# GpSimd's first weight splits of the second MoE moved into the second cross-attention, and those of the first expert taken from it

## The reference

```
x = x + L0_xattn(layernorm(x), ctx)      # 16 heads, null key, 1024 keys
x = x + L0_attn(layernorm(x))            # self-attention, 4 heads, q and k RMS-normed
x = x + L0_ffn(layernorm(x))             # mW1 = W1 + sum_e g_e TW1[e]; gelu; mW2 likewise: 8 experts mixed
x = x + L1_xattn(layernorm(x), ctx)      # 16 heads of 16, keys = context and own
x = x + L1_attn(layernorm(x))            # Mamba2 (residual inside), then memory retrieval and a gate
x = x + L1_ffn(layernorm(x))             # MoE: argmax routing over 8 experts, 256 -> 1024 -> 256
```

## Time and profile before

| | us |
|---|---|
| median of 3 runs | 514.2 (513.56 to 514.58) |
| span of the profiled execution | 512.5 |
| TensorE busy | 484.9 |
| VectorE busy | 261.0 |
| ScalarE busy | 232.9 |
| GpSimd busy | 80.2 |

### The profile page before, as it was taken

How to read it: one execution, slowest core, us unless ns; L and a number is a source line. 1 busy time by engine, 2 the same in 40 slices (tenths; PEclk the granted TensorE clock), 3 DMA queues, 4 the chain that set the end, 5 groups by cost and what they waited for, 6 DMA issues and landing times.

```text
span 512.5 us, 8527 instructions
## 1 busy us (share of the span) xinstructions
PE 484.9 (95%) x3600; PEld 414.8 (81%) x3600; DVE 261.0 (51%) x443; ACT 232.9 (45%) x409; POOL 80.2 (16%) x64
## 2 busy tenths in 40 slices
PE   6999999999999999999878999999999879889997
PEld 6977989899989999999765769975666669678697
DVE  2737131337065141420445977765656586467585
ACT  1636333346255141421125876516666253237772
POOL 2111000001010000000240434300000160203442
PEclk9989999999999999999999999999999999999999
DMA  8557000022420000000495999910000092255000
GB/s 320 223 193 243 2 2 0 1 83 83 165 82 1 1 0 1 1 2 1 157 425 234 388 420 405 366 70 1 2 1 1 1 373 121 84 212 199 0 1 10
DMA packets 12325, 62.50 MB, mean 122 GB/s; under 512 B 1183, under 2 KB 3615, under 8 KB 6400
## 3 DMA queue, kind: packets, MB, share of 16 engines
q1 hardware_dynamic: 9696, 52.17, 26.0%
q0 software_dynamic: 2592, 9.80, 5.5%
HBM read 61.84 MB, written 0.13 MB: 121 GB/s over the span
## 4 chain that ended last, share of the span: by engine, by line
PE 65%; issue 17%; DVE 8%; POOL 4%; ACT 3%; DMA 1%; POOLq 1%; SPq 0%; DVEq 0%; ACTq 0%
PE W L1322 18%; PE W L1283 14%; PE W L1466 8%; PE W L1513 6%; PE W L1264 3%; PE W L1299 3%; POOL w_lo L489 3%; PE W L1220 2%; PE W L1344 2%; POOL small L497 1%; DVE scr L1086 1%; ACT w_hi L552 1%; PE W L1458 1%; PE W L1383 1%; PE W L1247 1%
## 5 line engine op out<-in xcount | busy, mean ns | idle before, releaser
L1322 PE MATMUL W<-probs_turned_hi,ctx_split_hi 128*128 128x256 f32 x256 | 72.8, 284 | 0.1
L1322 PE MATMUL W<-probs_turned_hi,ctx_split_lo 128*128 128x256 f32 x256 | 72.4, 283 | 0.0
L1322 PE MATMUL W<-probs_turned_lo,ctx_split_hi 128*128 128x256 f32 x256 | 72.4, 283 | 0.0
L869 DVE TENSOR_TENSOR probs_turned_lo<-W,probs_turned_hi 128x512 fp32r<-128x512 f32 x32 | 20.6, 685 | 65.0 <-ACT probs_turned_hi L602 65.0
L1513 PE MATMUL W<-w_hi,acts 128*128 128x256 f32 x272 | 50.9, 286 | 1.5 <-DVE acts L836 1.0
L1283 PE MATMUL W<-ctx_turned_hi,q_keys_hi 128*128 128x512 f32 x128 | 51.7, 404 | 0.0
L1283 PE MATMUL W<-ctx_turned_hi,q_keys_lo 128*128 128x512 f32 x128 | 50.6, 395 | 0.0
L1283 PE MATMUL W<-ctx_turned_lo,q_keys_hi 128*128 128x512 f32 x128 | 50.6, 395 | 0.0
L1322 PEld LDWEIGHTS W<-probs_turned_hi,ctx_split_hi 128*128 128x128 f32 x256 | 49.1, 192 | 0.8 <-DVE probs_turned_lo L869 0.5
L1322 PEld LDWEIGHTS W<-probs_turned_lo,ctx_split_hi 128*128 128x128 f32 x256 | 49.1, 192 | 0.2
L1322 PEld LDWEIGHTS W<-probs_turned_hi,ctx_split_lo 128*128 128x128 f32 x256 | 49.1, 192 | 0.0
(11 more groups left out here) (347 smaller groups left out, 901.6 us busy)
## 6 DMA issues: line engine op xcount, KB each, us to landing
arena<-units_dram SPq DMA_DIRECT2D x22, 1024.0 KB, 8.0
ctxmem<-units_dram SPq DMA_DIRECT2D x16, 1024.0 KB, 10.1
fixed<-units_dram SPq DMA_DIRECT2D x7, 1024.0 KB, 6.8
scr<-ctx_dram POOLq DMA_DIRECT2D x4, 512.0 KB, 3.7
pbuf<-ctx_dram POOLq DMA_DIRECT2D x4, 512.0 KB, 5.3
ctxmem<-ctxT_dram SPq DMA_DIRECT2D x2, 1024.0 KB, 14.7
ctxmem<-ctx_dram SPq DMA_DIRECT2D x2, 1024.0 KB, 14.1
scr<-ctxT_dram POOLq DMA_DIRECT2D x3, 512.0 KB, 6.4
```

The source lines that it names most:

```text
L869: dve.tensor_tensor(PT[1][at], bank(4 + c).rearrange("p (t m) -> p t m", t=4), f32(PT[0][at]), ALU.subtract).then_inc(ev("pl_sb"), 1)
L1322: mm = pe.matmul(ps, CXN[a][:, t, c * P:(c + 1) * P], PT[z][:, t, :], start=(t == 0 and n == 0), stop=(t == KEYT - 1 and n == 2))
```

## The change

- Halves 0 and 1 (`f1e0`) no longer belong to GpSimd. ScalarE makes both high parts after its copy of q and k (L652), where it made one; VectorE makes both low parts, put behind the normalization of the probabilities (L965) and ahead of its wait for the attention's output (L968).
- The four halves of `m1e0` and `m1e1` stay with GpSimd, but stand behind n = 5 (the second cross-attention) and not behind n = 6 and n = 7 (the Mamba stage).

```diff
 def hi_maker(p):
-    return "gpsimd" if p == 0 or MOE0 <= p < MOE0 + SLOTS else "scalar"
+    return "gpsimd" if MOE0 <= p < MOE0 + SLOTS else "scalar"
 def lo_maker(p):
-    return "gpsimd" if hi_maker(p) == "gpsimd" or p == 1 or (p % 4 == 3 and p > SLOTS) else "vector"
+    return "gpsimd" if hi_maker(p) == "gpsimd" or (p % 4 == 3 and p > SLOTS) else "vector"
...
-                if n == RSQRT_QK:
-
-                    keep_w(0, 0)
-                    keep_w(1, 0)
-                    keep_w(1, 1)
...
+                    for p in range(MOE0, MOE0 + SLOTS):
                         keep_w(0, p)
                         keep_w(1, p)
+                if n == 6:
+
+                    pool.memset(XP[:, :, :, 0:TAPS - 1], 0.0).then_inc(ev("xp_zero"), 1)
...
-            keep_w_hi("f1e0", [1])
+            keep_w_hi("f1e0")
...
             ins.then_inc(*tick("probsA"))
+            keep_w_lo("f1e0")
             dve.wait_ge(*made("outA_ps"))
```

More of the change, by code:

```diff
@@ L524, in _ @@
                             .then_inc(ev("pads_zero"), 1)
+                    for p in range(MOE0, MOE0 + SLOTS):
+                        keep_w(0, p)
+                        keep_w(1, p)
                 if n == 6:
                     pool.memset(XP[:, :, :, 0:TAPS - 1], 0.0).then_inc(ev("xp_zero"), 1)
[L528 to L532, removed]
                 if n == N_RSQRT - 1:
```

## The result

| | before | after |
|---|---|---|
| median, first comparison (4 runs each) | 514.39 us | 509.8 us (508.81 to 510.38) |
| ratio, 95% interval | | 0.989 (0.9852 to 0.9928) |
| median, second comparison (23 and 5 runs) | 514.24 us | 509.74 us (509.31 to 510.38) |
| ratio, 95% interval | | 0.9912 (0.9897 to 0.9928) |
| span of the profiled execution | 512.5 us | 508.8 us |

The changed kernel is faster. Its median is the forecast 509.8 us. Its interval is wide: it holds the forecast ratio of 0.9914, and the two medians of its own row differ by 4.6 us only. The second comparison gives 0.9%.

A forecast was written before the change was run, and what follows sets the result against it. Mostly TensorE bounds the kernel, but small VectorE and ScalarE steps, some held by GpSimd splits, do in self-attention and Mamba. Gains of 1.25 + 0 + 3.15 = 4.4 us take 514.2 to 509.8 us, range 509.0 to 511.9.

The forecast's parts named there:

- Part A: Self-attention: without GpSimd's splits, L958 gains 0.34 us and the pair L965 0.91, together 1.25 us; added work is hidden.
- that rival: First expert stage is bound by transfers and gives back the self-attention's 1.25 us: time 511.1 us, chance 0.08.
- Part B: Second cross-attention: the eight moved GpSimd instructions hold up nothing that matters, L1036 included; cost 0.
- The nearest row: Rival, second cross-attention: L1036 stands still once like the 8-column L1077, costing 1.4 us; time 511.2 us, chance 0.20.
- Part C: Mamba stage: with the splits gone, L1067, L1077, L1078 and the L1086 round are no longer held; gain 3.15 us.
- TensorE's filler: Mamba stage: filling products, late next after VectorE's chain, would take less than 0.1 us of the gain.
- the last sentence of part C: TensorE's granted clock is 1.00 and the changed places only lose idle time, so the clock adds nothing.
- the sum: Whole kernel: 1.25 us from self-attention, 0 from second cross-attention, 3.15 us from Mamba, together 4.4 us less.
- The rival of the other sign: Second cross-attention: every VectorE instruction touching SBUF stands still beside a split, losing 4.9 to 9.8 us; chance 0.02.

The follow-up runs named there:

- e5: Changed kernel with an added 8-column VectorE TENSOR_SCALAR ahead of L1030 in the first two steps of the second cross-attention: 511.42 us.
- e6: Changed kernel with an added 1-column VectorE TENSOR_SCALAR ahead of L1030 in the first two steps of the second cross-attention: 509.91 us.
- e11: Kernel before with more filling products, 22 for 17 in the self-attention and 22 for 12 in the Mamba stage: 514.1 us, ratio 0.9959.
- the first part alone: Kernel before with only the first expert's split moved from GpSimd to ScalarE and VectorE, second-layer splits left in the Mamba stage: 514.15 us, ratio 1.0002.
- e1: The changed kernel itself, timed more often beside the kernel before: 509.74 us, ratio 0.9912.
- e4: Changed kernel with the fourth half's two instructions put back behind n = 7: 508.8 us, ratio 0.9899.
- e8: Changed kernel with VectorE making all low parts of the second products of both expert stages, where GpSimd made every fourth: 508.6 us, ratio 0.986.
- e9: Kernel before with only the first expert's split moved to ScalarE and VectorE, plus 22 for 12 filling products in Mamba: 512.79 us, ratio 0.9945.
- e12: Changed kernel with GpSimd making no low parts but those of the four moved halves, VectorE all others: 506.36 us, ratio 0.982 of the kernel before.
- e7: Changed kernel with fewer filling products, 14 for 17 in the self-attention and 9 for 12 in the Mamba stage: 510.44 us, ratio 0.9891.

## Why the prediction was right in its steps and wrong in its size

- Part A: 1.25 us forecast, 1.25 measured. The additions on ScalarE and VectorE were hidden. The first expert stage gave nothing back (65.40 us in both), so that rival is out.
- Part B: 0 forecast, 0 measured (73.12 and 73.11 us). The nearest row would have cost 1.4 us; e5 and e6 show that its 8 columns were the reason it was held, and that one column is not. Shown.
- Part C: 3.15 us forecast, 3.22 measured; the 0.07 is L1061, at 0.35 us instead of 0.43. TensorE's filler is what is late next, as said.
- The step that failed is the last sentence of part C: TensorE's clock is 1.00 in the rows and "the two changed places only lose idle time, so no term for the clock". The row that I read is that of the first expert stage, not of the changed places, and it is one execution, which I took for every execution. The idle stretches that the change removes (1.3 us in the self-attention, 2.5 in Mamba) put the kernel before at risk of losing a part of TensorE's clock. It has mean clocks under 0.997 in 5 of 23, 6 of 13 and 15 of 23 executions of three comparisons, 1 to 5 us above the others. Longer fillers in these two stretches took away all its executions above 515 us (e11) and 1.8 us of its median, 515.92 to 514.1. The whole change closes both stretches, and none of its nine executions has a mean clock under 0.993.
- So a term was missing that has no fixed size: by the comparisons it is between 0.2 us of the median (514.24 us with, 514.0 without the executions of lower clock) and 1.8 us, and the range's lower end should have been near 508. That it made the first ratio 0.989 is likely but not shown: one of the four executions of before in it is at 515.89 us, where others had 0.990, but their clocks are not on record. With 23 executions, most of full clock, the gain is 4.5 us (0.9912), beside the 4.4 of the sum. That the median came out at 509.8 to the tenth is in part luck, since the changed kernel's own executions spread from 508.8 to 510.4 us with the clock from 24 to 31 us, for which the sum had no term either.
- The rival of the other sign (all of VectorE's work held) is out: maxima and copies beside the splits are as long as before.

What stays open: why the first part alone has a mean clock of 0.990 to 0.993 in all twelve executions and the kernel before, with the same idle stretch, only in some. The runs differ in when the stretch comes, and no run varied that alone. How often the kernel before loses it differs between the comparisons (5 of 23 with e1 to e4, 6 of 13 with e5 to e8, 15 of 23 with e9 to e12), which ran on three different chips; nothing here tells chip from chance. No execution of the kernel before at 515 us or more was profiled, so where it lost the clock is told by e11 and not by a trace. Nor is it shown what makes the low clock from 24 to 31 us shorter or longer between kernels that are the same there, nor what the rest of the 1.8 us is.

## What to carry to other kernels

Before work is given to GpSimd, look at what VectorE does beside it: an instruction with two SBUF inputs, or a TENSOR_SCALAR between SBUF tiles of more than one column, stood still here until GpSimd's ended, while PSUM sources, reductions and single columns passed. Move GpSimd's work beside the latter. An edit that shortens a wait of TensorE can have a second worth that one profile does not show: ask of every idle stretch in both versions whether the clock survives it in all executions, and never price two edits from runs of each alone when both touch such stretches.

## What the runs showed of the hardware

- An instruction of 8 numbers per partition was held for 1.1 us and one of 1 number for nothing, at the same point of the same GpSimd subtraction.
- TensorE lost its clock after idle stretches as short as 0.69 us (e7, with two more waits of 0.68 and 0.47 us close behind it), and kept it in other executions after 2.51 us. The length of the one stretch does not decide it.
- Filling products in a wait cost nothing and took 0.4% off the kernel before (e11).
- The clock from 24 to 31 us was 0.51 in one profiled execution and 0.76 in two others with the same instructions there; the lower one cost 1.2 to 1.4 us.
- GpSimd's subtraction of 128x1024 took 2.35 us in the cross-attention and 3.57 us beside VectorE's subtractions; VectorE's own took 1.22 us with none beside it.
